# First attention of a fused transformer kernel: all row-tile scores of a step before its full-array work on TensorE

## The reference

```
x = layernorm(hidden) * ln_w + ln_b
q, k, v = x @ Wq + bq, x @ Wk + bk, x @ Wv + bv     # 16 heads of 8
q, k = l2norm(q), l2norm(k)
state = q
for _ in range(2):
    att = softmax(state @ k^T)                       # per head, 256 x 256
    state = att @ v
return residual + state @ Wo + bo
```

## Time and profile before

| what | value |
|---|---|
| median of 3 runs | 1450.89 us (1449.8 to 1456.36) |
| profiled execution, first to last instruction | 1467.2 us |
| TensorE matmul busy | 1305.1 us, 89% |
| VectorE busy | 1130.4 us, 77% |
| ScalarE busy | 969.6 us, 66% |
| GpSimd busy | 751.3 us, 51% |
| mean granted TensorE clock | 0.954 |

### The profile page before, as it was taken

The page is one execution under the profiler, slowest core; times in us unless marked ns, Lnnn a source line. Parts: engine busy times, 40 slices in busy tenths (PEclk is TensorE's granted clock), DMA queues, the critical chain, the costliest instruction groups (busy, mean ns, idle before and its releaser), DMA issues. The chain is left out here.

```text
span 1467.2 us, 34194 instructions
## 1 busy us (share of the span) xinstructions
PE 1305.1 (89%) x12121; PEld 987.2 (67%) x12121; DVE 1130.4 (77%) x3054; ACT 969.6 (66%) x1498; POOL 751.3 (51%) x961
## 2 busy tenths in 40 slices
PE   2899999999998689899927999999999998699997
PEld 1566666666654367899915777777777776588886
DVE  5578889889875667899956888888888776567776
ACT  1688888888886447777723777777777777343441
POOL 4775665787852363799866455455444220101112
PEclk9899999999998779999958999999999999799999
DMA  6000000111111021122121111111111110134353
GB/s 234 18 23 20 22 20 20 28 32 28 31 36 30 8 80 32 56 73 73 58 87 51 49 47 48 46 48 47 49 46 38 39 42 18 26 92 116 80 129 82
DMA packets 84430, 77.20 MB, mean 53 GB/s; under 512 B 18224, under 2 KB 72240, under 8 KB 83888
## 3 DMA queue, kind: packets, MB, share of 16 engines
q1 hardware_dynamic: 80176, 66.73, 17.1%
q0 software_dynamic: 4096, 8.40, 2.0%
HBM read 36.26 MB, written 13.63 MB: 34 GB/s over the span
## 5 line engine op out<-in xcount | busy, mean ns | idle before, releaser
L541 ACT ACTIVATE a_p<-a_ps_s 128x1024 f32<-128x1024 f32 x256 | 258.3, 1031 | 25.1 <-PE a_ps_s L400 22.2
L651 DVE TENSOR_REDUCE a_qt<-a_ps_d 128x2 fp32r<-128x512 f32 x256 | 174.6, 687 | 48.9 <-PE a_ps_d L411 44.9
L1298 DVE TENSOR_REDUCE a_qt<-a_ps_d 128x2 fp32r<-128x512 f32 x256 | 173.3, 688 | 44.9 <-PE a_ps_d L1086 39.9
L822 POOL TENSOR_TENSOR a_rn<-a_ss,a_half 128x16 f32<-128x16 f32 x56 | 162.6, 2920 | 1.3
L1203 ACT ACTIVATE a_pg<-a_ps_s 128x1024 f32<-128x1024 f32 x128 | 125.8, 1024 | 26.8 <-PE a_ps_s L1075 25.4
L418 PE MATMUL a_ps_o<-a_p,a_v 128*32 128x256 f32 x2048 | 129.5, 393 | 3.7 <-ACT a_p L541 3.7
L1086 PE MATMUL a_ps_d<-a_kpad,a_qs 128*128 128x512 f32 x256 | 126.0, 495 | 5.8 <-DVE a_qt L1298 2.7
L411 PE MATMUL a_ps_d<-a_kpad,a_qs 128*128 128x512 f32 x256 | 126.8, 496 | 4.3 <-DVE a_qt L651 2.4
L2300 ACT ACTIVATE f_s<-f_ps_g 128x512 f32<-128x512 f32 x72 | 43.0, 598 | 99.9 <-PE f_ps_g L2246 99.7
L1494 POOL DMA_INDIRECT a_picked<-ys,rows x64 | 67.6, 1056 | 61.8 <-PE a_ps_d L1086 50.8
L418 PEld LDWEIGHTS a_ps_o<-a_p,a_v 128*32 128x32 f32 x2048 | 61.2, 112 | 52.9 <-issue 22.3
(11 more groups left out here) (355 smaller groups left out, 3823.9 us busy)
## 6 DMA issues: line engine op xcount, KB each, us to landing
a_kpad<-a_kc SPq DMA_DIRECT2D x512, 32.0 KB
f_gb<-spread SPq DMA_DIRECT2D x64, 256.0 KB, 5.7
a_kpad<-a_kq SPq DMA_DIRECT2D x256, 32.0 KB, 1.8
f_xin<-xs SPq DMA_DIRECT2D x39, 128.0 KB, 2.1
ys<-f_yout SPq DMA_DIRECT2D x39, 128.0 KB, 2.1
w<-in_w SPq DMA_DIRECT2D x2, 2304.0 KB, 11.4
out_x<-X SPq DMA_DIRECT2D x8, 256.0 KB, 6.8
xs<-f_zero SPq DMA_DIRECT2D x15, 128.0 KB
```

Source lines behind the costliest of these rows:

```text
L541: nc.scalar.activation(probs[:, u % 2, 2 * c:2 * c + 2, :, :].rearrange("p a b c -> p (a b c)"), ps_s[:, 2 * c:2 * c + 2, :].rearrange("p ...
L651: nc.vector.tensor_reduce(qt2[:, (k - PEAK) % 4, 2 * part:2 * part + 2, SHIFT], bank(k, f"m{part}")[:, :].rearrange("p (a b) -> p a b", b= ...
L822: nc.gpsimd.tensor_tensor(rn[:, part * c:(part + 1) * c], ss[:, part * c:(part + 1) * c], half[:, 0:c], ALU.pow).then_inc(rn_ready, 1)
L1298: nc.vector.tensor_reduce(qt[:, b % 2, GLOBAL, n:n + 2, SHIFT], bank(k, f"m{part}")[:, :].rearrange("p (j s) -> p j s", s=S), AX.X, ALU.ma ...
```

## The change

On TensorE S2 moves up to stand right behind At, and m0 and yT move down to stand behind S2. A step's list becomes: `op`, S1, At, S2, m0, `yT`, `xT`, `qp`, m1, m2, T, `lg`, m3, `kp`, `zT`, `vp`, O, KQ. On ScalarE exp2 moves ahead of the copy of xT, and the copy of yT, which stood between exp0 and exp1, moves behind exp2. The orders of `ps_a` and `ps_d`, the buffers, the instructions and their number stay as they are.

```diff
@@ TensorE @@
                     scores(k, q_of(k))
-                if unit(k - PEAK):
-                    u = k - PEAK
-                    pe.wait_ge(kpad_loaded[u % PAD_RING], 64 * (u // PAD_RING + 1))
-                    pe.wait_ge(a_done, a_count(k - 1, "T"))
-                maxima(st, 0)
-                if a_live(k, "yT"):
-
-                    pe.wait_ge(d_done, d_count(k - 1, "O"))
-                    wait_a(st, "yT")
-                    transposes(ps_a, lambda t: out2[:, b % 2, t, :], a_full)
                 if unit(k - 1) or unit(k - LAST_USE):
...
                     last.then_inc(o_full, 1)
+                if unit(k - SECOND):
+                    pe.wait_ge(exp_done, exps_of(k, 1))
+                    pe.wait_ge(a_done, a_count(k - 1, "T"))
+                    scores(k - SECOND, qs2[:, (k - 1) % 2, S:2 * S])
+                if unit(k - PEAK):
+                    u = k - PEAK
+                    pe.wait_ge(kpad_loaded[u % PAD_RING], 64 * (u // PAD_RING + 1))
+                    pe.wait_ge(a_done, a_count(k - 1, "T"))
+                maxima(st, 0)
+                if a_live(k, "yT"):
+
+                    pe.wait_ge(d_done, d_count(k - 1, "O"))
+                    wait_a(st, "yT")
+                    transposes(ps_a, lambda t: out2[:, b % 2, t, :], a_full)
                 if a_live(k, "xT"):
...
                 maxima(st, 1)
-                if unit(k - SECOND):
-                    pe.wait_ge(exp_done, exps_of(k, 1))
-                    pe.wait_ge(a_done, a_count(k - 1, "T"))
-                    scores(k - SECOND, qs2[:, (k - 1) % 2, S:2 * S])
                 maxima(st, 2)
@@ ScalarE @@
                     exps(st, 0, k, p1)
-                if a_live(k, "yT"):
-                    copy_a(st, "yT", yT[:, :])
                 if unit(k):
                     exps(st, 1, k, p1)
...
                     nc.scalar.copy(ot[:, live], ps_o[:, live]).then_inc(o_copied, 1)
+                if unit(k - SECOND):
+                    exps(st, 2, k - SECOND, p2)
+                if a_live(k, "yT"):
+                    copy_a(st, "yT", yT[:, :])
                 if a_live(k, "xT"):
...
-                if unit(k - SECOND):
-                    exps(st, 2, k - SECOND, p2)
```

More of the change, by code:

```diff
@@ L455, in _ @@
                     scores(k, q_of(k))
+                if unit(k - 1) or unit(k - LAST_USE):
+                    wait(pe, o_copied, attends(k - 1))
+                    pe.wait_ge(exp_done, exps_of(k - 1, 3))
+                    if unit(k - LAST_USE):
+                        last = attend(k - LAST_USE, p2, 1)
+                    if unit(k - 1):
+                        pe.wait_ge(v_ready, k)
+                        last = attend(k - 1, p1, 0)
+                    last.then_inc(o_full, 1)
+                if unit(k - SECOND):
+                    pe.wait_ge(exp_done, exps_of(k, 1))
+                    pe.wait_ge(a_done, a_count(k - 1, "T"))
+                    scores(k - SECOND, qs2[:, (k - 1) % 2, S:2 * S])
                 if unit(k - PEAK):
@@ L465, in _ @@
                     transposes(ps_a, lambda t: out2[:, b % 2, t, :], a_full)
[L466 to L474, removed]
                 if a_live(k, "xT"):
```

## The result

The kernel after takes 1514.36 us (median of 4 runs, 1513.36 to 1515.66), the one before 1450.93 us (median of 4). The ratio is 1.0424, 95% interval 1.0397 to 1.0451: 63 us slower. The prediction said 1524, with 1490 to 1552 as its range: slower, as forecast, by 63 us instead of 73.

A forecast was written before the change was run, and what follows sets the result against it. TensorE's matmuls were taken to set the step, ScalarE's exponentials right behind. 59 steps at 1.26 us (+74), other steps +4 and hidden routing -5 gave +73 on 1450.89: 1524 us, range 1490 to 1552.

The forecast's parts named there:

- four maxima in line on two banks: Steps r = 0, 1, 3: m2, m3 and O wait for VectorE's maxima; +1.3, +1.3 and +1.05 us a step.
- the chain of yT and xT: Steps r = 2: yT's copy behind exp2 delays xT, m1 and T; next S1 at 8.15 against 6.77, +1.4 us.
- the ladders: Start times forecast link by link within a step: next S1 at 7.65, 7.61, 8.15 and 8.6 us for r = 0 to 3.
- What is removed: Each step: six changes of array tiling become four, 0.09 us each, 0.18 saved; 0.15 if nothing takes their place.
- changes are dear: Two tiling changes removed per step outweigh the new waits if each costs 0.63 us; at most 1442 us; 4%.
- S2's wait for exp1: Step r = 1: S2 needs exp1 until 2.63, so TensorE waits 0.3 us where m0 and m1 stood.
- The first rival: Only ScalarE's T copy and exp3 lengthen each step, maxima do not gate: +0.7 us a step, 1492 us; 10%.
- The count of steps: First attention: 59 full steps (k = 5 to 63) lose a mean of 1.26 us each, +74 us.
- the -5: Router's choosing and placing on VectorE, four times: partly hidden in free time before m0's maximum, -5 us (0 to -10).
- What was put at nothing: Three sublayers after the first attention start later but are unchanged: 0 us.
- that sign: Prediction counts as wrong if the granted clock leaves 1.00 in the middle of the first attention.
- its rival on the clock: TensorE's idling lowers the clock; 15 steps lose some 2.5 us each, 38 us more, 1562 us; 7%.

## Why the prediction was right, and where its terms were off

The mechanism was right: four maxima in line on two banks for r = 0, 1 and 3, the chain of yT and xT for r = 2. The sizes were too large, mostly those of the ladders and of the late steps; the price of a change of tiling was too small.

- **What is removed.** The kinds of change that stay cost what was taken: S1 to At 0.44, as S1 to m0 was; At to S2 1.86 where it does not wait, as At to m1 was. But 0.09 for a change that goes was misread. The prediction took m2 to T, 0.34, as the price of staying on the full array, and m2 itself stands right behind row tiles. With m0 back, two such matmuls stand together, and from 363.99 to T at 364.56 they take 0.57: 0.34 for the one behind row tiles, 0.23 for the one behind it. So a matmul between tiles (0.43) costs 0.20 more than one that stays. The steps with r = 1 agree: with m0 back, one change fewer, T comes 3.74 after S1 (360.82 to 364.56) instead of 3.94; with m0 alone moved it comes at 3.92, of which 0.18 is m2 coming late behind S2 (0.62 instead of 0.44). Two changes are worth 0.40 a step, not 0.18. The sentence in the Trainium skill ("TensorEngine Tiling (Array Packing)", Key Properties) that a change of mode drains TensorE may describe what happens. The gain does not reach the time, since in the new order waits set the steps: with m0 alone moved, one change fewer came with +21 us. The rival "changes are dear" wanted 0.63 for a change and is out.
- **S2's wait for exp1.** Forecast 0.3; the row shows 0.22 idle, and S2 starts 0.29 later than it could. It is a part of the loss, since m0, and with it VectorE's line of maxima, starts behind it: 0.29 of the 1.13 and 0.96 for r = 0 and 1, by an estimate (29 such steps) 8 us. The early S2 alone is not slow: with short maxima and T early it waits 0.22 as well, and r = 1 takes 6.14, less than the 6.29 before.
- **Maxima in a row on two banks, r = 0, 1 and 3.** This was the main term, and the runs bear it out from three sides: 37 us by moving m0 back, 38 us by shortening the maxima, 5 us by shortening them before. It was too large. For r = 1 the step was forecast at 7.61 and is 7.25. The prediction read 1.48 us between the maxima of m0 and m1 in the earlier trace rows as VectorE's own work. But m1 itself came at 315.63, and its maximum 0.54 later, at 316.17: the row showed m1's arrival. In line, VectorE needs 1.33 (353.29 to 354.62). Back-to-back maxima also start nearer 0.6 apart (1.28 for two) than the 0.68 taken, and KQ takes 0.53 (356.45 to 356.98), not 0.61. For r = 0 and 3 the forecast of 7.65 and 8.6 met 7.46 and 8.41 for the last two reasons.
- **The chain of yT and xT, r = 2.** Forecast 8.15, measured 8.07. Short maxima left this step at 8.03, m0 back left it at 8.28; so it is another mechanism than the banks. What putting yT back would give was misjudged (the wait for VectorE's output), so it is not shown by a cure, only by the idle time in the row. The last link was not exp3: it ended 7.85 into the step (363.80 + 1.03 less 356.98) and would have let S1 go at 7.99; S1 came at 8.07, right behind KQ and the output projection, which the ladder for r = 2 had left out.
- **ScalarE's chain, T copy and exp3.** The first rival gave it as the only limit. For r = 1 it is the second one: with the banks relieved it holds the next S1 by 0.30, and with T early as well, the step falls by 0.4.
- **The count of steps.** 59 steps were taken as full, but from step 52 on no new sequence is projected, and those lose 0.61, not 1.26. For them the forecast had 12 x 1.26 = 15 us, and 7 were lost. For the other 47 it had 59, and 49.5 were lost (1.05 each), because the ladders were too long. So nearly half of the error of the steps is the count. Some of the router's work was hidden, as the -5 has it: steps 28 to 52, with two rounds of it, lose 24.1 us without the 2.6 of the granted clock (below), and six times 4.23 (four steps without a round) is 25.4. That is 1.3 for two rounds.
- **What was put at nothing.** The three sublayers behind took 2.5 us more (955.5 against 953.0). The cause is open.
- **The clock.** The granted clock was 1.00 in most steps, but not in all: between steps 28 and 52 four had 0.88, 0.90, 0.90 and 0.91 (steps 44, 45, 49 and 50; two below), while before all were at 1.00. They took 8.33, 7.61, 9.35 and 8.54 us where their like took 7.46, 7.25, 8.48 and 8.07, together 2.6 us of the 26.65. The prediction had called itself wrong if the clock left 1.00 in the middle of the stage; it did, so that sign came up, and its rival on the clock is right in kind, at a small part of the 38 us that it was given. In the ordinary steps TensorE stood idle less than the rival took: 1.25 us of 7.25 for r = 1 (7.25 less 6.00 busy).

```profile
373.46:381.79 8.33, 7.22 (x69) 4.74 (x68) 6.01 (x25) 5.46 (x7) 5.69 (x6) 0.88 0.08 22
413.35:422.70 9.35, 7.84 (x74) 5.22 (x73) 7.10 (x32) 5.45 (x7) 5.05 (x5) 0.90 0.10 22
```

Not tried: a third bank for `ps_d`. The tensors of the code hold eight banks already (`ps_s` four, `ps_o`, `ps_a`, `ps_d` two), so the banks were relieved by shorter reads instead.

## What to carry to other kernels

A task that seems to interrupt a neat sequence on one engine can be the cover for a reader on another: before grouping like with like, write down for each buffer of the group how long its reader takes and how many buffers there are, and put that ladder beside the price of the switch. Here four producers with 0.69 us readers and two buffers wanted to be spread over the step, and 0.40 us of switches was no match for waits that made the step 1.1 us longer. What is put in front of the first producer counts in full, since the line of readers starts only behind it. When reading the distance between two instructions on an engine, ask whether the second waited for its input, since an idle time too short to be printed looks like work. And when two distances are compared for the price of a switch, ask whether the cheaper one has a switch in it as well.

## What was not expected of the hardware

A 128x512 matmul on the full array took TensorE 0.43 between tiles, 0.34 right behind row tiles and ahead of full-array work, and 0.23 with full-array work on both sides. Column tiles followed by row tiles cost nothing more than column tiles followed by the full array (At to S2 1.86, At to m1 1.86), and row tiles to column tiles 0.44, like row tiles to full array. The row maximum over 64 instead of 256 keys, two groups each, took 0.29 instead of 0.69 us: 0.40 us for 384 elements fewer. A straight line through the two, an estimate, leaves 0.16 us that does not depend on the length.
